# A two-layer transformer kernel: global keys along the diagonal and global values as moving operand in the second attention

## The reference

```python
Q, K, V = (x @ W.T + b).reshape(B, 256, 16, 8)            # for each of the three
s_loc = Q . K[l-32 .. l+32] * scale                       # window of 65 keys, softmax, times V
local = softmax(s_loc) @ V[window]
Kg, Vg = K[:, global_indices], V[:, global_indices]       # 25 global keys
glob  = softmax(Q . Kg * scale) @ Vg
out   = (0.7 * local + 0.3 * glob) @ Wo.T + bo
```

## Time and profile before

| what | value |
|---|---|
| median of three runs | 1113.35 us |
| the profiled execution | 1111.69 us |
| its span, first to last instruction | 1109.9 us |
| granted TensorE clock, mean | 0.929 |
| first attention | about 25 to 325 us |
| one-expert mixture | about 325 to 450 us |
| second attention | about 450 to 870 us |
| top-2 mixture | about 900 to 1110 us |

### The profile page before, as it was taken

The page is one execution under the profiler, slowest core; times in us unless marked ns, Lnnn a source line. Parts: engine busy times, 40 slices in busy tenths (PEclk is TensorE's granted clock), DMA queues, the critical chain, the costliest instruction groups (busy, mean ns, idle before and its releaser), DMA issues.

```text
span 1109.9 us, 27990 instructions
## 1 busy us (share of the span) xinstructions
PE 961.9 (87%) x7664; PEld 709.4 (64%) x7664; DVE 784.3 (71%) x3615; ACT 578.1 (52%) x1250; POOL 681.8 (61%) x1491
## 2 busy tenths in 40 slices
PE   2999999999959995899999999999999419999950
PEld 1777777777734552677777777777776317877730
DVE  3788888888826786457776878777776327888845
ACT  2466676666621432255555555555555107777734
POOL 3566666666631222266768787888878623777765
PEclk9899999999978998599999999999999659999985
DMA  6121211111032442121112121222111157777717
GB/s 182 27 52 27 49 40 35 45 30 45 23 133 88 170 152 86 29 49 28 47 29 59 38 59 37 60 55 59 52 40 36 43 177 226 240 252 245 234 56 212
DMA packets 71376, 98.36 MB, mean 89 GB/s; under 512 B 13688, under 2 KB 43256, under 8 KB 71104
## 3 DMA queue, kind: packets, MB, share of 16 engines
q1 hardware_dynamic: 61040, 83.31, 25.6%
q0 software_dynamic: 4992, 10.30, 2.7%
q10 hardware_dynamic: 5232, 3.42, 1.2%
HBM read 49.48 MB, written 24.77 MB: 67 GB/s over the span
## 4 chain that ended last, share of the span: by engine, by line
PE 74%; DVE 9%; issue 6%; SPq 3%; DMA 3%; POOL 2%; ACT 2%; DVEq 0%; ACTq 0%; POOLq 0%
PE bank L348 6%; PE bank L172 5%; PE bank L253 4%; PE bank L357 4%; PE bank L378 4%; PE bank L1499 4%; PE bank L1500 4%; PE bank L1501 4%; PE bank L1265 4%; PE bank L412 4%; PE bank L419 3%; PE bank L168 3%; PE bank L352 3%; PE bank L387 3%; PE bank L404 2%
## 5 line engine op out<-in xcount | busy, mean ns | idle before, releaser
L536 ACT ACTIVATE p<-bank 128x480 f32<-128x480 f32 (+1 forms) x448 | 240.4, 540 | 256.3 <-PE bank L378 101.0
L671 DVE CUSTOM_DVE_ANT_0 bank<-bank,band 128x160 f32<-128x160 f32 x512 | 157.1, 348 | 80.7 <-PE bank L348 67.9
L671 DVE CUSTOM_DVE_ANT_0 bank<-bank,causal 128x128 f32<-128x128 f32 (+1 forms) x512 | 169.8, 388 | 56.4 <-PE bank L352 40.6
L901 POOL TENSOR_SCALAR_AFFINE_SELECT p<-p 128x380 f32<-128x380 f32 (+1 forms) x256 | 146.6, 602 | 63.2 <-ACT p L536 62.3
L1677 POOL DMA_INDIRECT y_rows<-p,rows x92 | 108.3, 1177 | 64.0 <-DVE p L1630 42.7
L671 DVE DVE_READ_ACCUMULATOR2_ANT nm<- 128x1 f32 x1024 | 145.5, 142 | 0.1
L882 POOL TENSOR_SCALAR_AFFINE_SELECT p<-p 128x256 f32<-128x256 f32 (+1 forms) x192 | 91.1, 486 | 69.1 <-ACT p L536 64.2
L348 PE MATMUL bank<-ks,qs 128*128 128x186 f32 x512 | 116.2, 311 | 3.1 <-issue 1.6
L348 PEld LDWEIGHTS bank<-ks,qs 128*128 128x128 f32 x512 | 79.6, 196 | 35.9 <-issue 21.0
L378 PE MATMUL bank<-qs,ks 128*128 128x160 f32 x512 | 100.4, 299 | 0.0
L1570 ACT ACTIVATE p<-bank,wb 128x512 f32<-128x512 f32 x92 | 63.6, 691 | 39.4 <-PE bank L1501 24.3
(11 more groups left out here) (209 smaller groups left out, 2369.0 us busy)
## 6 DMA issues: line engine op xcount, KB each, us to landing
qs<-parts SPq DMA_DIRECT2D x46, 512.0 KB
qs<-qf SPq DMA_DIRECT2D x128, 128.0 KB, 2.4
rows<-xr SPq DMA_DIRECT2D x23, 260.0 KB
parts<-ks SPq DMA_DIRECT2D x8, 512.0 KB
xs<-x_b SPq DMA_DIRECT2D x16, 256.0 KB
p<-in_w SPq DMA_DIRECT2D x12, 256.0 KB
xin<-in_x SPq DMA_DIRECT2D x16, 128.0 KB, 2.2
parts<-qf SPq DMA_DIRECT2D x4, 512.0 KB
```

The source lines that it names most:

```text
L536: act.activation(pb[:, :, :].rearrange("p u c -> p (u c)")[:, lo:lo + cols], bank[:, 0:cols], ACT.Exp, scale=SCALE).then_inc(L.exp_done, 1)
L671: return dve.tensor_tensor_reduce(at, at, mask, -1.0, -BIG, ALU.add, ALU.min, nm[:, item:item + 1])
L901: pool.affine_select(out=at, in_=at, compare_op=ALU.is_ge, fill=0.0, base=base, pattern=[[0, 4], [sign, hi - lo]], channel_multiplier=-sig ...
```

## The change

- The queries are kept stacked as well: three tiles `T.qf` in turn, and SyncE writes the maxima's rows into them beside `qs` (a second small DMA for each step). `mrow` counts 32 a batch in place of 16.
- The global keys `T.kg` become [128, 4, 128] fp32r, with the keys of group j on rows 32j to 32j+31 and columns 32j to 32j+24 only. One matmul with K = 128 and 128 columns gives the global scores of four heads (all groups of one t). Unit 3 exists only in steps 2 and 3 and does two t each, 256 queries moving. So an iteration has 14 second-pass units and not 16 (`unit2` numbers them).
- The exponential of unit 3 goes over 512 columns into `T.pg[j - 2]`.
- `pv` part 2 and the round `og` are gone. In step 0, unit 0 of the iteration after, `global_values` has the exponentials stationary (128 queries) and 64 columns of `vgb` moving, eight times, and gives the result with the queries on the partitions, where `normalise` reads it. `ogs` is not copied any more.
- `keep_vg` is one product in place of four; `keep_kg` signals after the two copies and again after four small additions. `pass1(0, 0)` waits for the first signal only.
- Bank 0 no longer holds `og`; mx0 follows pj0. Bank 1 is as it was.
- SyncE may spread the next queries after unit 2 of step 2.
- The new tiles share memory with the row buffers of the last stage; GpSimd clears the larger `kg`.

```diff
-ROUNDS = (("pj0", "og", "mx0", "ont", "mx1", "y", "q1", "xt", "mx3"),
+ROUNDS = (("pj0", "mx0", "ont", "mx1", "y", "q1", "xt", "mx3"),
           ("rp", "ot", "pj1", "rt", "q0", "vg", "rl", "mx2", "k0", "k1", "kg"))
...
+    def pass2_unit(self, local, j, u):
+        if local and u == 3:
+            return self.late and j > 1
+        return self.pass2[j] and u < 3
...
+        def global_values():
+
+            pe.wait_ge(L.exp_done, L.unit2(i - 1, 3, 3) + 1)
+            pe.wait_ge(L.vg_kept, fin + 1)
+            wait(pe, L.on_done, fin)
             for tau in range(2):
-                for r in range(2):
-                    m = turn(T.mi[0][:, (2 * tau + r) * P:(2 * tau + r + 1) * P],
-                             T.ogs[:, r, tau * P:(tau + 1) * P])
-            m.then_inc(L.ot_done, 1)
+                out = T.og[:, tau * S:(tau + 1) * S].rearrange("p (r t z) -> p r t z", r=2, t=4)
+                for t in range(4):
+                    m = pe.matmul(out[:, :, t, :], T.pg[t // 2][:, t % 2 * S + tau * P:t % 2 * S + (tau + 1) * P],
+                                  T.vgb[p][:, t, :].rearrange("p (r z) -> p r z", r=2),
+                                  start=tau == 0 and t == 0, stop=True, skip_group_check=True)
+            m.then_inc(L.pg_done, 1)
...
             if L.local and u == 3:
-                for t in range(4):
-                    m = pe.matmul(bank[32 * t:32 * t + 32, 0:S], T.kg[par][:, t, :], q[:, t, :].bitcast(F32),
-                                  start=True, stop=True)
+                pe.wait_ge(L.kg_kept, 2 * i)
+                for c in range(2):
+                    t = 2 * (j - 2) + c
+                    m = pe.matmul(bank[:, c * S:(c + 1) * S], T.kg[n][:, t, :], T.qf[(i - 1) % 3][:, t, :],
+                                  start=c == 0, stop=True, skip_group_check=True)
...
-            if part == 2:
-                if j == 0:
-                    pe.wait_ge(L.vg_kept, i)
-                pe.wait_ge(L.exp_done, 4 * step + 4)
-                m = pe.matmul(T.og[:, r * S:(r + 1) * S], T.vgb[n][:, j, :], pb[:, 3, 0:S],
-                              start=j == 0, stop=False, skip_group_check=True)
...
-                if j == 0 and u == 2 and th.finish and L.local:
-                    round_og()
+                if j == 0 and u == 0 and th.finish and L.local:
+                    global_values()
...
+            if L.local and u == 3:
+                wait(act, L.pg_done, i - 1)
+                act.activation(T.pg[j - 2], bank[:, :], ACT.Exp, scale=SCALE).then_inc(L.exp_done, 1)
+                return
...
-                dve.tensor_copy(T.ks[n][:, :, lo:lo + NGE], kg[:, :, 0:NGE])
-            dve.tensor_scalar(T.kg[n][:, :, 0:NG], kg[:, :, 0:NG], T.rows[:, 0:1], None,
-                              ALU.add).then_inc(L.kg_kept, 1)
+                m = dve.tensor_copy(T.ks[n][:, :, lo:lo + NGE], kg[:, :, 0:NGE])
+            m.then_inc(L.kg_kept, 1)
+            for j in range(4):
+                own = slice(32 * j, 32 * j + 32)
+                m = dve.tensor_scalar(T.kg[n][own, :, 32 * j:32 * j + NG], kg[own, :, 0:NG], T.rows[own, 0:1], None, ALU.add)
+            m.then_inc(L.kg_kept, 1)
...
+                if L.local:
+                    qf = T.qf[(i - 1 if j == 0 else i) % 3]
+                    sp.dma_start(qf[32 * js + 24:32 * js + 24 + L.parts, :, :].bitcast(F32),
+                                 T.mt[js][0:4 * L.parts, :].bitcast(F32)).then_inc(L.mrow[js], 16)
```

More of the change, by code:

```diff
@@ L53, in __init__ @@
         self.parts = 4 if local else 2
-        self.kept = 2 if local else 1
+        self.rows_sent = 32 if local else 16
         def s(what):
@@ L91, in __init__, with unit2 @@
             self.steps = 22
+    def unit2(self, i, j, u):
+        if not self.local:
+            return 3 * (4 * i + j - 3) + u
+        if i == 0:
+            return u
+        return 3 + 14 * (i - 1) + (0, 3, 6, 10)[j] + (u if j < 3 or i < B else u - 3)
 class There:
@@ L174, in in_iteration @@
     def in_iteration(name, i, p, th):
-        if name in ("og", "vg", "kg", "rt", "rl", "rp") and not L.local:
+        if name in ("vg", "kg", "rt", "rl", "rp") and not L.local:
             return False
@@ L209, in bank_read @@
             "k1": (L.k_kept, 2 * k + 4), "xt": (L.xt_kept, k + 3),
-            "vg": (L.vg_kept if L.local else None, k + 1), "kg": (L.kg_kept if L.local else None, k + 2)}[last]
+            "vg": (L.vg_kept if L.local else None, k + 1), "kg": (L.kg_kept if L.local else None, 2 * k + 4)}[last]
         wait(pe, signal, value)
@@ L363, in pass2 @@
             par, batch = (n, i - 1) if j < 3 else (p, i)
-            unit = L.units * (4 * i + j - 3) + u
-            bank = T.s2[u % 2 if L.local else (j + u) % 2]
+            unit = L.unit2(i, j, u)
+            bank = T.s2[unit % 2 if L.local else (j + u) % 2]
             if u == 0:
-                pe.wait_ge(L.mrow[js], L.q_base + 16 * batch + 16)
+                pe.wait_ge(L.mrow[js], L.q_base + L.rows_sent * (batch + 1))
             wait_apart(pe, L.passed, L.exp_done, unit - L.ring2 + 1)
@@ L425, in pv @@
                                       start=False, stop=False, skip_group_check=True)
-            if part == L.kept:
+            if part == 1:
                 m.then_inc(L.pv_done, 1)
@@ L458, in body @@
                     round_mx(j)
-                if th.pass2[j]:
+                if th.pass2_unit(L.local, j, u):
                     pass2(j, u)
-                if th.late and u > 0:
+                if th.late and u in (1, 2):
                     pv(j, u - 1)
@@ L483, in keep_pv @@
             if not (isinstance(i, int) and i == 2):
-                act.wait_ge(L.ot_done, L.kept * fin)
+                act.wait_ge(L.ot_done, fin)
             act.copy(T.ovs[:, :, :], T.ov[:, :].rearrange("p (r q) -> p r q", r=2)).then_inc(L.ov_kept, 1)
-            if L.local:
-                act.copy(T.ogs[:, :, :], T.og[:, :].rearrange("p (r q) -> p r q", r=2)).then_inc(L.ov_kept, 1)
         def keep_xt(batch):
@@ L524, in keep_stack @@
                     wait(act, q_in, L.q_base + 16 * (i + 1))
-                act.copy(T.qf[:, :, tau * P:(tau + 1) * P], from_).then_inc(L.q_kept, 1)
+                qf = T.qf[(i + 1) % 3 if L.local else 0]
+                act.copy(qf[:, :, tau * P:(tau + 1) * P], from_).then_inc(L.q_kept, 1)
         def exp(j, u):
@@ L529, in exp @@
             pb = T.p[(j + 1) % 2]
-            bank = T.s2[u % 2 if L.local else (j + u) % 2]
-            cols = (S if u == 3 else len(local_items(u)) * WIN) if L.local else 512
-            act.wait_ge(L.p2_done, L.units * step + u + 1)
+            unit = L.unit2(i, j, u)
+            bank = T.s2[unit % 2 if L.local else (j + u) % 2]
+            act.wait_ge(L.p2_done, unit + 1)
+            if L.local and u == 3:
+                wait(act, L.pg_done, i - 1)
+                act.activation(T.pg[j - 2], bank[:, :], ACT.Exp, scale=SCALE).then_inc(L.exp_done, 1)
+                return
+            cols = len(local_items(u)) * WIN if L.local else 512
             if u == 0:
                 wait(act, L.pv_done, step - 1)
-            lo = 3 * WIN * u if L.local and u < 3 else 512 * u
+            lo = 3 * WIN * u if L.local else 512 * u
             act.activation(pb[:, :, :].rearrange("p u c -> p (u c)")[:, lo:lo + cols], bank[:, 0:cols], ACT.Exp,
```

81 lines of the change are left out of this document (41 added, 40 removed).

## The result

The changed kernel takes 1169.08 us (median of four runs, 1165.17 to 1174.16), the kernel before on the same chip 1113.61. The ratio is 1.0514, with a 95% interval from 1.0479 to 1.0549: 55.5 us slower by the medians, where +6 was forecast. The profiled execution took 1171.72 us around a span of 1170.0, 60.1 more than before, and its mean granted clock was 0.865 in place of 0.929. Two executions each of e5 and e10, the profiled ones among them, and one of e6 took over 1.5% longer than the fastest of their kernel; they are left out of the ratios and times, and the traces of e5 and e10 are read for mechanisms only.

The account below looks back on a forecast made before the run. The order of dependent work across engines was taken as the bound, though PE was busy 49.41 of 50 us. Even and odd iterations +9.5, early and last ones -3.0, total +6.5 us: 1119 us, range 1099 to 1128.

Parts of the forecast that it names:

- slower: Outcome case: the changed kernel over 0.5% slower than the kernel before; chance 0.35.
- the same: Outcome case: within 0.5% (5.6 us) of the kernel before, 1107.8 to 1118.9 us; chance 0.40.
- The new matmuls: Eight f32 global-value matmuls, 16 instructions in step 0 ahead of unit 2: 0.115 us each, 1.85 us per iteration.
- The price ahead of T: From first score matmul (t0) to the normalisation's last add (T): new matmuls add their whole 1.85 us, removals there shorten nothing.
- The forecast wait for the add: PE stands waiting for the normalisation's last add in every iteration with a projection, 1.2 to 1.6 us.
- Iterations 2 and 3: Early iterations without scatters on GpSimd or routing on VectorE: -0.6 us each.
- iteration 1: Second iteration, which has none of the new global-value matmuls: about -2.2 us.
- iteration 0: First iteration, which has one global step less: -0.8 us.
- The gain behind T: From the normalisation's last add to the next iteration's first score matmul: -0.55 to -0.6 us even, -1.1 odd.
- keep_kg's four small adds: VectorE's four adds in place of one: about +0.8 us, costed at nothing as covered by idle time and the new matmuls.
- rival 4: Clock falls from t0 to T, doubling 5 us of PE work: +56 us in 14 iterations, 1175 us; chance 0.05.
- the rival that it was taken from: Whole PE saving is had behind T: -0.6 us for 14 iterations, -3 at the edges, 1102 us; chance 0.2.

Follow-up runs that it names:

- e5: The changed kernel with filler matmuls in all four places where TensorE idles over 0.5 us; 1142.49 us, ratio 1.028.
- e10: The changed kernel with the second attention's layer norm moved behind the copies of the gathered keys; 1160.66 us, ratio 1.0442.
- e6: The changed kernel with GpSimd's sum of input and bias (xb) in step 0 in place of step 2; ratio 1.0579.
- e4: The kernel before with eight dummy f32 matmuls where the change has its global-value matmuls; 1140.61 us, ratio 1.0302.
- e2: The changed kernel with 10 in place of 4 filler matmuls at an iteration's end and 4 ahead of step 1; ratio 1.0608.
- e3: The changed kernel with the global-value matmuls at the end of the iteration before, in place of the eight filler instructions; 1131.63 us, ratio 1.0196.
- e13: e12 without any of its three added fills; 1132.67 us, ratio 1.0206.
- e12: The changed kernel with e3's move, xb in step 0, the layer norm behind the key copies, and fillers at three places; 1100.51 us, ratio 0.9916.
- e7: e3 with GpSimd's sum of input and bias (xb) also moved to step 0; ratio 1.0272.

## Why the prediction was wrong

The forecast leaned to slower, but "the same" had the larger chance (0.40 against 0.35); the size was wrong by 50 us, and the range did not hold the time. By its steps:

- *The new matmuls*, 0.115 us each, 1.85 an iteration: right in size. L248 starts 726.98, the next group 1.70 later (0.106 each); at full clock t0 to T grows by 1.86 (even).
- *The price ahead of T is paid whole*: right, and e4 shows it in the kernel before (+1.78). The forecast wait for the add came too: 1.39 us (forecast 1.2 to 1.6).
- *Iterations 2 and 3*: 23.38 and 23.39 us against 24.27, so -0.9 (forecast -0.6); iteration 1 -3.4 (forecast -2.2), iteration 0 only -0.1 (forecast -0.8). Where neither routing nor scatters fill VectorE and GpSimd, the shorter PE list did pay.
- *The gain behind T, -0.55 to -0.6 even and -1.1 odd*: the first step that failed. It was 0.05 the other way for the even ones, and 18.26 against 18.31 for the odd one of e5. In the odd ones a part of it was there: i = 11 of the kernel after does its part behind T in 17.82 us, 0.5 less than 18.31, though 3.1 us of it are at the lower level. I had followed GpSimd's xb up to VectorE's residual, and no further: on PE the turning behind step 2 waits for that residual (up to 1.0 us here, 2.0 in e2 and e3), and e6 got the 0.6 of the even iteration when xb came early. And I had costed VectorE's operations by their durations in the old neighbourhood. The layer norm had already taken 2.77 and 2.17 us in place of 0.6 in two iterations of the kernel before, ahead of its only two late starts (0.47 and 1.15 us); in the new order it does so more often (up to 2.60), ahead of the key copies for which the next t0 waits. e10 got 1.2 us of it back.
- *keep_kg's four small adds, about +0.8, covered*: the size was near (1.31 for the four in place of 0.32), the cover failed. The four adds write what nobody needs at t0, but the router's round in the odd iterations stands behind them on its bank: 0.5 to 0.8 us of wait in every odd iteration from i = 5 on. In e5 this wait alone stands ahead of falls of the clock.
- *The clock, rival 4, chance 0.05*: this is the largest failure. The forecast had the clock at 1.00 and gave its loss no term in the sum; it was 0.83 over 500 to 850 us. The size of the rival was 1175 against 1169; the odd iterations do from t0 to T what it said of all. That the two numbers lie so close is luck, since its mechanism was half right: the long falls do not begin at the new matmuls and the wait at T (in the kernel after a fall that begins there lasts 3.4 us), but at the idle places at the start of odd iterations. The rival named the wait at T, but its chance was set by the 0.20 us of wait and the router's matmuls of the kernel before, and the idle time that must come when 2.5 us of PE work go from an iteration that gets no shorter was not in it.
- *The range*: its lower end, 1099, is 3 us below the 1102 of the rival that it was taken from; this changes nothing here.

How the 60.1 us of span divide can be reckoned up to the t0 of i = 15 (875.42 after, 829.15 before: +46.3). At the upper level, by after's even iterations and e5's odd one: the six even ones from i = 4 on +9.9 (1.3, four times 1.9, 1.0), the five odd ones +8.3 (1.1 to 1.8 each), iterations 0 to 3 -5.3, the start of the stage -2.3: +11. The other 35 are put down to the clock, by subtraction. With 17.82 in place of e5's 18.26 the odd ones would cost about 2 us less, so 11 is rather too much and 35 rather too little. Dead work gave back as much in size: 32 us from e13 to e12, 26 from the change to e5. The last 13.8 us lie behind that t0, 7 of them in i = 15, which runs t0 to T at the lower level; the rest I did not divide.

What stays open: what decides whether the clock falls behind a given idle place. e5 fell behind the router's 0.75 us alone, e10 and e13 with less idle time than the change has; but the kernel before passed 0.47 us once and 1.15 us once without a fall, and no run varied one gap alone. Why e7 is slower than e3 is not explained beyond its lower clock, and why moving the layer norm or xb shows no gain without fill likewise rests on that alone. Nor was it tried to swap keep_kg's two halves between banks, so that the router's round would not wait.

## What to carry to other kernels

In this kernel work taken off TensorE was a gain only where TensorE's list set the end of the stretch; elsewhere it became idle time, and idle places of 0.75 to 2.1 us could cost the clock, which here cost about three times what the order did. So when a change shortens a full PE list, forecast its gaps, find the old filler, and price the clock falling as a likely case. Follow each cross-engine chain to the end (xb, residual, turning), and take no duration of a VectorE operation for given if GpSimd's work beside it moves.

## What the runs showed of the hardware

- In the kernel after the upper clock level was lost behind one or two idle places within 4 us, none longer than 2.13 us, and it stayed lost for 3.4 to 27 us; in e5 behind a single wait of 0.75 us, for 13.7 us. The same idle time was also passed without a fall (1.39 us at T in five iterations of the kernel after, 1.15 us in the kernel before). With dead f32 matmuls in the gaps the clock of the stage was higher (0.90 in e13, 0.98 in e12). One fall each of e12, e3, e7 and e13 began where PE had been busy for 3.7 to 3.8 of the 4 us ahead; they lasted 3.4 us, and I have no cause for them.
- An f32 matmul with 128 stationary and 64 moving columns takes two instructions, 0.11 us each, whether behind real data (L248) or the identity (e4), and 16 in a row in e4 left the clock at 1.00.
- Two `tensor_scalar` of 128 x 128 f32 on VectorE took 0.6 us alone and up to 2.8 beside a string of GpSimd's masks (2.77 in the kernel before, 2.60 in the kernel after); a single one took 0.34 alone and up to 2.4 (2434 ns in the kernel before).
- A VectorE `tensor_scalar` on 32 partitions and 100 elements took 0.32 us in the kernel after (L651), as much as one on 128 partitions and 100 elements in the kernel before (L633): four block-wise writes cost four times one.
